# Gated sliding-window attention on one core: queries and keys projected transposed, rotated as pair components and placed by transfers inside SBUF

## What is computed

```python
q = jnp.einsum('bqm,muh->bquh', hidden_states, Wq) + bq
k = jnp.einsum('bkm,mvh->bkvh', hidden_states, Wk) + bk
v = jnp.einsum('bkm,mvh->bkvh', hidden_states, Wv) + bv
q = _interleaved_rope(q, cos, sin) * SCALE   # (even*cos - odd*sin, odd*cos + even*sin)
k = _interleaved_rope(k, cos, sin) * SCALE
scores = jnp.einsum('bquh,bkuh->buqk', q, k)           # k, v repeated over the 4 heads of a group
scores = jnp.where(jnp.abs(pos[:, None] - pos[None, :]) <= 128, scores, NEG)
probs = softmax(concat([scores, sinks]))[..., :-1]
out = jnp.einsum('buqk,bkuh->bquh', probs, v)
x = x + (jnp.einsum('bquh,uhm->bqm', out, Wo) + bo) * silu(fp8(xn) @ w.T + bias)
```

## Time and profile before

| | |
|---|---|
| median of 3 runs | 1935.78 us (1932.91 to 1942.27) |
| profiled execution: span, first to last instruction | 1928.5 us |
| TensorE busy with matmuls | 1818.4 us (94%) |
| VectorE, ScalarE, GpSimd busy | 1373.2, 1406.3, 1183.6 us |
| mean granted TensorE clock | 0.983 of full speed |

### The profile page before, as it was taken

One profiled execution on the slowest core, in us unless ns is written; L12 is line 12 of the kernel. 1 busy time (PEld: TensorE's weight loads), 2 busy tenths in 40 slices (PEclk: granted clock), 3 DMA queues, 4 the chain that ended last, 5 costly groups with the idle time before them and its releaser, 6 DMA issues.

```text
span 1928.5 us, 48655 instructions
## 1 busy us (share of the span) xinstructions
PE 1818.4 (94%) x13199; PEld 1707.6 (89%) x13199; DVE 1373.2 (71%) x4883; ACT 1406.3 (73%) x3764; POOL 1183.6 (61%) x1511
## 2 busy tenths in 40 slices
PE   3499999999999999999999999999999999999997
PEld 2399998999989999899989999899998999889996
DVE  8776776777767777767767777577777676776775
ACT  3277777777767777777867777677877787777775
POOL 4465656666566666666656666566666665665654
PEclk9699999999999999999999999899999999999999
DMA  5200000000000000000000000000000000000000
GB/s 191 82 8 2 0 1 25 12 2 0 13 20 5 1 0 18 19 2 0 1 19 18 2 0 1 30 7 2 0 18 19 2 1 1 18 24 2 0 1 17
DMA packets 20889, 28.07 MB, mean 15 GB/s; under 512 B 1344, under 2 KB 19264, under 8 KB 20544
## 3 DMA queue, kind: packets, MB, share of 16 engines
q1 hardware_dynamic: 20672, 25.45, 4.0%
HBM read 21.25 MB, written 4.19 MB: 13 GB/s over the span
## 4 chain that ended last, share of the span: by engine, by line
PE 86%; DVE 5%; issue 4%; ACT 1%; DMA 0%; DVEq 0%; POOLq 0%; POOL 0%; ACTq 0%
PE pv_bank L1042 26%; PE ring L974 15%; PE ring L1016 10%; PE acc L1063 9%; PE score L1028 8%; PE score L1030 7%; PE ring L983 5%; PE ring L1051 3%; PE ring L995 2%; PE ring L964 1%; PE ring L1001 1%; DVE junk L772 1%; DVE neg_max L781 1%; DVE sink_arg L786 1%; DVE proj L760 1%
## 5 line engine op out<-in xcount | busy, mean ns | idle before, releaser
L1042 PEld LDWEIGHTS pv_bank<-v,stage 128*128 128x128 f32 x5136 | 682.5, 192 | 4.7 <-issue 1.1
L1042 PE MATMUL pv_bank<-v,stage 128*128 128x65 f32 x5136 | 674.0, 266 | 0.9 <-DVE o_norm L800 0.9
L772 DVE CUSTOM_DVE_ANT_0 junk<-ring,mask 128x384 bf16<-128x384 f32 (+1 forms) x1036 | 507.0, 490 | 224.9 <-PE ring L1016 198.3
L529 ACT ACTIVATE stage<-score 128x512 f32<-128x512 f32 x640 | 357.0, 588 | 283.1 <-PE score L1030 282.3
L464 POOL TENSOR_SCALAR_AFFINE_SELECT stage<-stage 128x512 f32<-128x512 f32 x384 | 243.2, 641 | 425.1 <-ACT stage L529 425.1
L1016 PE MATMUL ring<-kT_high,qT_full 128*128 128x384 f32 (+1 forms) x1036 | 398.9, 385 | 16.6 <-DVE proj L760 15.4
L444 POOL TENSOR_TENSOR qk_parts<-turned,qk_parts 128x320 fp32r<-128x320 f32 x263 | 227.3, 864 | 207.0 <-ACT qk_parts L564 207.0
L552 ACT ACTIVATE qT_high<-ring,own_rows 8x128 fp32r<-8x128 f32 x1032 | 284.9, 345 | 13.7 <-PE ring L1001 7.3
L1028 PE MATMUL score<-qT_full,kT_high 128*128 128x512 f32 x640 | 267.7, 418 | 16.1 <-issue 14.9
L760 DVE TENSOR_TENSOR proj<-ring,bias 128x384 f32<-128x384 f32 x264 | 145.7, 552 | 183.7 <-PE ring L974 183.2
L1030 PE MATMUL score<-qT_high,kT_low 72*128 72x512 f32 x640 | 256.3, 400 | 0.0
(11 more groups left out here) (110 smaller groups left out, 3282.4 us busy)
## 6 DMA issues: line engine op xcount, KB each, us to landing
x_in<-in_x SPq DMA_DIRECT2D x13, 512.0 KB, 3.6
x_res<-in_x SPq DMA_DIRECT2D x18, 256.0 KB, 3.3
out<-x_res SPq DMA_DIRECT2D x16, 256.0 KB, 2.2
stage<-in_w_qkv SPq DMA_DIRECT2D x4, 768.0 KB, 5.0
...
```

The lines of the kernel that those rows point to most:

```text
L529: nc.scalar.activation(prob[:, q % 2 * 3 + n, :], score[(FIRST[q] + n) % 2][:, :], ACT.Exp) \
L772: nc.vector.tensor_tensor_reduce(junk[:, h % 2, 0:cols], ring[h % 2][:, 0:cols], mask[:, m0:m0 + cols], 1.0, LOWEST, ALU.add, ALU.max, row ...
L1042: last = nc.tensor.matmul(pv[:, h, :], prob[:, q % 2 * 3 + n, h * P:(h + 1) * P], v[:, par, k, :], start=(n == 0), stop=(n == len(BLOCKS[q ...
```

## The change

**Projection.** The weights are reordered on the host so that one product gives, for one group, the even components of its 4 heads (4 x 32 = 128 rows) by 512 tokens, a second one the odd components (`queries`, 2 x 6 products of 512 columns a step). Keys are made for four groups at once (`W_K`), twice a batch; values for all eight groups at once, one tile of tokens at a time (`project_values`), 4 times a batch. Nothing has to be turned by TensorE; `turn_q_full` and `turn_k` go.

**Rotation.** The even and odd tiles are rotated as wholes: ScalarE takes them out with their bias (`even_out`, `odd_out`), GpSimd does four products and two sums of 128x512 and two more for the low parts, ScalarE rounds two high parts.

**Placement.** The result has head h on partitions 32h to 32h+31, while the score products want one head's 64 components on partitions 0 to 63 and its high parts on 64 to 127. SyncE moves them by DMA from SBUF to SBUF: 24 transfers of 32 partitions x 512 numbers (64 KB each) for the queries of a step, 6 for its keys. `qT_full` and `qT_high` have two slots for groups, `kT_high` and `kT_low` three.

**Maxima.** They are negated, turned and written out for two tiles at a time: `turn_max` for tiles 0 and 1 in tile 2 of the step before the group's own, for tiles 2 and 3 in tile 0 of its own.

**Loops.** All steps are written out; the loops and their register arithmetic are gone. The residual input has a buffer for the whole batch, and one batch less is loaded and normalised at the start.

```diff
+            def keys_in(t):
+                quad, r = t // QUAD, slice(t % QUAD * HALF, (t % QUAD + 1) * HALF)
+                sp.wait_ge(s_k_lo, 2 * quad + 2)
+                upto(sp, s_score_pe, NB * (t - 2))
+                upto(sp, s_kT_in, K_IN * t)
+                for row, part in ((0, k_first_hi), (HALF, k_second_hi), (D, k_first_hi), (D + HALF, k_second_hi)):
+                    sp.dma_start(kT_high[row:row + HALF, t % 3, :].bitcast(F32), part[r, :]).then_inc(s_kT_in, 16)
+                for row, part in ((0, k_first), (HALF, k_second)):
+                    sp.dma_start(kT_low[row:row + HALF, t % 3, :].bitcast(F32), part[r, :]).then_inc(s_kT_in, 16)
+            def queries_in(a, row, low, high, ready, done):
+                sp.wait_ge(ready, a + 1)
+                upto(sp, s_score_pe, NB * (a - 1))
+                upto(sp, done, Q_IN * a)
+                for h in range(GROUP):
+                    r = slice(h * HALF, (h + 1) * HALF)
+                    sp.dma_start(qT_full[row:row + HALF, a % 2, h, :].bitcast(F32), low[r, :]).then_inc(done, 16)
+                    sp.dma_start(qT_full[D + row:D + row + HALF, a % 2, h, :].bitcast(F32), high[r, :]) \
+                        .then_inc(done, 16)
+                    sp.dma_start(qT_high[row:row + HALF, a % 2, h, :].bitcast(F32), high[r, :]).then_inc(done, 16)
...
+            def step(it):
+                n, k = it // KV, it % KV
...
+                if real(t) and t % QUAD:
+                    keys_in(t)
+                if k == 0 and n >= 1:
...
+                if real(t) and t % QUAD == 0:
+                    keys_in(t)
+                if real(a):
+                    queries_in(a, 0, q_first, q_first_hi, s_first_lo, s_qT_first_in)
+                    queries_in(a, HALF, q_second, q_second_hi, s_second_lo, s_qT_second_in)
...
+            def turn_even(a):
+                pool.wait_ge(s_even_done, a + 1)
+                upto(pool, s_qT_first_in, Q_IN * a)
+                upto(pool, s_qT_second_in, Q_IN * a)
+                nc.gpsimd.tensor_tensor(q_first[:, :], q_even[:, :], cos[:, :], ALU.mult).then_inc(s_rope, 1)
+                nc.gpsimd.tensor_tensor(q_second[:, :], q_even[:, :], sin[:, :], ALU.mult).then_inc(s_rope, 1)
+            def turn_odd(a):
+                pool.wait_ge(s_odd_done, a + 1)
+                nc.gpsimd.tensor_tensor(q_second_hi[:, :], q_odd[:, :], sin[:, :], ALU.mult).then_inc(s_rope, 1)
+                pool.wait_ge(s_rope, 6 * a + 3)
+                nc.gpsimd.tensor_tensor(q_first[:, :], q_first[:, :], q_second_hi[:, :], ALU.subtract) \
+                    .then_inc(s_rope, 1)
+            def turn_rest(a):
+                nc.gpsimd.tensor_tensor(q_odd[:, :], q_odd[:, :], cos[:, :], ALU.mult).then_inc(s_rope, 1)
+                pool.wait_ge(s_rope, 6 * a + 5)
+                nc.gpsimd.tensor_tensor(q_second[:, :], q_second[:, :], q_odd[:, :], ALU.add).then_inc(s_rope, 1)
+            def first_low(a):
+                pool.wait_ge(s_first_hi, a + 1)
+                nc.gpsimd.tensor_tensor(q_first[:, :], q_first[:, :], q_first_hi[:, :], ALU.subtract) \
+                    .then_inc(s_first_lo, 1)
+            def second_low(a):
+                pool.wait_ge(s_second_hi, a + 1)
+                nc.gpsimd.tensor_tensor(q_second[:, :], q_second[:, :], q_second_hi[:, :], ALU.subtract) \
+                    .then_inc(s_second_lo, 1)
...
-            def q_full(b, q):
-                at(act, s_qfull_pe, TILES, b, q + 1)
-                nc.scalar.activation(qT_full[:, q, :], ring[0][:, :], ACT.Copy).then_inc(s_qfull_done, 1)
...
+            def even_out(a):
+                act.wait_ge(s_q_pe, 2 * a + 1)
+                upto(act, s_rope, 6 * (a - 1) + 2)
+                nc.scalar.activation(q_even[:, :], ring[1][:, :], ACT.Identity,
+                                     bias=q_bias[:, a % KV * 2:a % KV * 2 + 1]).then_inc(s_even_done, 1)
+            def odd_out(a):
+                act.wait_ge(s_q_pe, 2 * a + 2)
+                upto(act, s_rope, 6 * a)
+                nc.scalar.activation(q_odd[:, :], ring[1][:, :], ACT.Identity,
+                                     bias=q_bias[:, a % KV * 2 + 1:a % KV * 2 + 2]).then_inc(s_odd_done, 1)
...
+            def max_rows(s, pair):
+                act.wait_ge(s_max_turned_pe, 2 * s + pair + 1)
                 for h in range(GROUP):
-                    last = nc.scalar.activation(qT_high[D:D + NR, q, h * P:(h + 1) * P], ring[2][0:NR, 0:P],
-                                                ACT.Copy, scale=own_rows[:, h:h + 1])
+                    last = nc.scalar.activation(qT_high[D:D + NR, s % 2, h, pair * 2 * P:(pair + 1) * 2 * P],
+                                                ring[2][0:NR, 0:2 * P], ACT.Copy, scale=own_rows[:, h:h + 1])
                 last.then_inc(s_max_rows_done, 1)
...
+            def keys_turn(quad, odd):
+                dve.wait_ge(s_k_pe, 2 * quad + odd + 1)
...
+                    upto(dve, s_kT_in, K_IN * QUAD * quad)
+                    parts = ((k_first, cos), (k_second, sin))
+                for dst, turn in parts:
+                    nc.vector.scalar_tensor_tensor(dst[:, :], ring[1][:, :], b, turn[:, :], ALU.add, ALU.mult) \
+                        .then_inc(s_k_turned, 1)
...
+            def values(m, t):
+                dve.wait_ge(s_v_pe, TILES * m + t + 1)
+                last = KV - 1 + m % 2
+                nc.vector.tensor_tensor(v[:, 0:KV - 1, t, 0:D],
+                                        ring[1][:, 0:(KV - 1) * D].rearrange("p (g d) -> p g d", d=D),
+                                        v_bias[:, 0:(KV - 1) * D].rearrange("p (g d) -> p g d", d=D), ALU.add)
+                nc.vector.tensor_tensor(v[:, last, t, 0:D], ring[1][:, (KV - 1) * D:], v_bias[:, (KV - 1) * D:],
+                                        ALU.add).then_inc(s_v_done, 1)
...
+            def negated(s, pair):
+                g, i = s % KV, 2 * s + pair
+                dve.wait_ge(s_max_done, TILES * GROUP * s + 2 * GROUP * (pair + 1))
+                upto(dve, s_sink_done, i - 1)
...
+                nc.vector.scalar_tensor_tensor(neg_max[:, :, :], row_max[:, pair, :, :], -1.0, n_s, ALU.mult, ALU.min) \
                     .then_inc(s_small_self, 1)
...
+            def project(col, done):
+                products = [(w, xs, k) for k in range(KT)
+                            for w, xs in ((w_hi, xT_hi), (w_lo, xT_hi), (w_hi, xT_lo))]
+                for n, (w, xs, k) in enumerate(products):
+                    last = nc.tensor.matmul(ring[1][:, :], w[:, k, col:col + P], xs[:, k, :], start=(n == 0),
                                             stop=(n == len(products) - 1))
-                last.then_inc(s_proj_pe, 1)
-
...
+            def queries(a, odd):
+                if odd:
+                    pe.wait_ge(s_even_done, a + 1)
...
+                project(W_Q + (a % KV * 2 + odd) * P, s_q_pe)
...
+            def turn_max(s, pair):
+                pe.wait_ge(s_neg_done, 2 * s + pair + 1)
+                upto(pe, s_max_rows_done, 2 * s + pair)
+                for t in range(2):
+                    last = nc.tensor.matmul(ring[2][0:NR, t * P:(t + 1) * P], neg_parts[:, pair, t, :], ident_r[:, :],
+                                            start=True, stop=True)
+                last.then_inc(s_max_turned_pe, 1)
...
+            def score_rows(b, q, h, it):
+                if q == 0 and h == 0:
+                    pe.wait_ge(s_qT_first_in, Q_IN * (b + 1))
+                    pe.wait_ge(s_qT_second_in, Q_IN * (b + 1))
+                    pe.wait_ge(s_kT_in, K_IN * (b + 1))
...
+                upto(pe, s_max_done, TILES * GROUP * b + GROUP * q + h - 1)
+                k0, cols = window(q)
+                nc.tensor.matmul(ring[h % 2][:, 0:cols], qT_full[:, b % 2, h, q * P:(q + 1) * P],
+                                 kT_high[:, b % 3, k0 * P:k0 * P + cols], start=True, stop=True).then_inc(s_max_pe, 1)
...
+                    if q == 0 and real(it + 2):
+                        queries(it + 2, 0)
+                    if real(it):
+                        scores(it, q, 0)
+                        scores(it, q, 1)
+                    if q == 0 and real(it + 2):
...
+                    if other is not None:
...
+                        scores(it, q, 2)
+                    row(0)
+                    weighed(0)
+                    maxima_turn()
+                    if it == -1 and q == 3:
+                        largest()
+                    row(1)
+                    weighed(1)
+                    weighed(2)
+                    row(2)
+                    heads_turn()
+                    weighed(3)
+                    row(3)
+                    if real(c3[0]):
+                        out_project(*c3)
```

1186 lines of the change are left out of this document (534 added, 652 removed).

## The result

The changed kernel takes 2551.97 us (median of 4 runs, 2550.87 to 2565.38) against 1937.19 (1932.91 to 1942.27): a ratio of 1.322, interval [1.316, 1.329]. The forecast was 2110 us, the range 1900 to 2270. The direction was right and the size was not: 442 us are missing, nearly all of them in the length of a step.

What follows compares the result with a forecast made beforehand. TensorE's work and SyncE's transfers alternate in each step: 17.05 + 12.6 + 0.4 + 1.2 = 31.25 us. 85 + 63.8 x 31.25 + 23.4 = 2102 us of span, so 2110 us expected, range 1900 to 2270.

Steps and rivals of the forecast that it cites:

- TensorE sets the time before, 28.36 us a step: TensorE's own work bounds the kernel before; if it stayed the limit, the changed step would be 25.8 us.
- W: TensorE's work from a step's first row product to its last score: 16.3 us, 17.05 with 0.75 of stalls.
- V: TensorE's other work beside the transfers, between the last score and the next step's first row product: 8.7 us.
- The ring: TensorE's work up to the last score and the transfers after it cannot overlap; TensorE idles 3.9 us a step.
- L: From last score through 24 transfers to the next step's first row product: 12.6 us; late new keys add 0.4.
- interval of 0.45 us: Time between SyncE's issues of the query transfers; 23 intervals make 10.35 us, ends 0.37 and 0.54.
- Clock, 1.2 us a step: TensorE at half clock after each step's idle gap, 2.4 us a step: costs 1.2 us, ends 0 and 3.4.
- GpSimd hides ahead of T: GpSimd's 13.4 us of query rotation end before T, the last score, costing nothing; with new keys SyncE is 1.6 late.
- S: Start of a step's first row product, where GpSimd's rotation also starts.
- Head 85 us: Time before the first score: 85 us instead of 95.9, ends 76 and 96.
- The first: Rival, chance 0.10: the transfers fit beside TensorE's other work, step 25.8 us, 1761 us in all.
- The third: Rival, chance 0.10: longer interval or landing and low clock, transfer stretch 15.5 us, step 35.15, 2360 us in all.

Runs made afterwards that it cites:

- e9: Changed kernel with 18 of a group's 24 query transfers left out from the third step on: 1879.82 us, ratio 0.972 to the kernel before.
- e16: Changed kernel with queries written to HBM and read back in six pieces, new keys issued between, row products one tile later: 1875.84 us, ratio 0.971.
- e2: Changed kernel with the 12 transfers of the second components issued on ScalarE's queue instead of SyncE's: 2056.75 us, ratio 1.065 to the kernel before.
- e4: Changed kernel with the 8 transfers a step into qT_high left out from the third step on: 2218.7 us, ratio 1.150 to the kernel before.
- e1: Separate kernel, only copying x and issuing groups of 12 transfers in nine forms: SBUF to SBUF 0.63 to 0.66 us apart, HBM to SBUF 0.46.
- e3: Changed kernel with 12 to 46 useless products a step on TensorE ahead of the first row product: 2471.78 us, ratio 1.281 to the kernel before.
- e5: Changed kernel with three slots of qT_full and qT_high, two of each staging tile, low parts of weights not kept: 2197.66 us, ratio 1.141.
- e7: e2 with SyncE's first 30 transfers put behind one more load of x and of weights in the start-up: 2058.97 us, ratio 1.067.

## Why the prediction was right in kind and wrong in size

- *TensorE sets the time before, 28.36 us a step.* Nothing contradicts it. But the count of what the change takes from it was too good. Forecast for a TensorE-bound step: 25.8 us. e9 and e16 show 27.6 and 27.4. The change takes 0.7 to 1.0 us a step, not 2.6. W had 16.3 of work and 0.75 of stalls; without transfers it is 18.1 (e9), and V is 9.5, not 8.7. The pieces that the change touches were sized well: the projection takes 4.4 us a step, forecast 4.3, and the turned queries and keys that went took 2.27, forecast 2.24. What was carried over unchanged did not stay so. With each product counted up to the next one's start, over 59 middle steps, e9 against before has 1.44 us a step without any product against 0.61, and for as many products as before 0.99 against 0.71 (turned heads), 8.33 against 8.05 (values), 0.45 against 0.29 (maxima), 3.68 against 3.54 (rows). That is 1.7 of the 1.8 us. Some 0.3 of it, an estimate, is the clock (0.98 against 0.99 from 200 to 1800 us); why the rest grew is not shown.
- *The ring.* Right. It binds: 12 issues moved away took 495 us off (e2), 8 left out 333 us (e4), 18 left out 672 us (e9). That TensorE waits at L1080 in each step, for the transfers, is right, 62 times 8.3 us where the forecast had 4. One sign of being wrong that the prediction named did show in part: SyncE's queue is held by another wait, 15 times by `k_second` (301.6 us). It matters in two steps of eight, under L.
- *L = 12.6 + 0.4 of keys.* Mis-sized: 17.9. The step that failed is this term, and in it the **interval of 0.45 us**: it was taken from loads out of HBM, as no row showed SBUF at both ends, and I argued from size ("the form here is smaller than any of these") where e1 shows that size plays no part. 23 x (0.632 - 0.45) = 4.2 us of the 4.9. The upper end, 0.54, was the rows' and not the form's. The rest is an issue that now and then takes 1.4 us (once in about three steps), and the keys: 3.1 us in two steps of eight, 0.8, not 0.4. The landing of 2.0 us was right (2.0 in the page's part 6, 2.09 to the row product with its wake).
- *Clock, 1.2 us a step.* Low: 1.6 by e3 (20.4 - 18.8) to 2.3 by e9 (20.4 - 18.1). The reason was right: a stretch at 0.50 after a gap, of 8 us in the step shown. The filler did not bring it back wholly, so 1.6 is a lower bound. W as a whole, forecast at 17.05 + 1.2, is 20.4.
- *GpSimd hides ahead of T.* Right in plain steps, with 1.27 to 1.30 us for each operation, though not by the count: its last operation on the queries ends 16.7 us after S, not 13.4, which T = S + 17.05 would just have hidden and the longer W hides well. With new keys SyncE issues the first of them at S + 18.7, not 15.9, and the queries at S + 22.7, not 18.6. With the third slot GpSimd is the next bound (e5).
- *Head 85 us.* Wrong in sign: 114.2, against 95.9. TensorE waits there 22 us for `q_even` and 21 for the first transfers. I counted work that left and not the 30 transfers and the ScalarE copies that came; of the transfers e7 moved some back without a gain. Tail 16.0, not 23.4.
- *The sum.* 63.8 x (37.93 - 31.25) = 426 us, head +29, tail -7: 448 us between the forecast's span, 2102, and 2550.4. The interval alone is 4.2 us a step, some 270 us; with that and nothing else put right the forecast would still be 170 us short, and W is most of what is left. The 7.3 us added for what lies around the span were too many: each run's time stands 1.6 to 1.9 us above its own span (2552.13 against 2550.4), and the rest was the difference between one execution and the median of others.
- *Rivals.* The first, transfers hidden beside TensorE's work, is out: an interval of 0.63 is over twice its border of 0.28. What it drew on, the Trainium skill's remark on the sequencer's time in DMA: Bandwidth & Descriptors, does not hold for this size: 0.63 us from issue to issue (e1) against the prediction's estimate of 0.20 us of movement. The third, the longer ring, was the nearest, at 0.10, with L = 15.5 and a step of 35.15, and its own interval of 0.54 still too short. "SBUF at both ends costs more than a row shows" should have been an end of the range with an open top.
